# Seeding the attention score banks from ScalarE: three matmul passes instead of four in a post-layernorm transformer block

## The reference, cut to what matters

```python
q, k, v = (hn @ W + b).reshape(b, s, 16, 64)      # q and k then get the rotary embedding
attn = einsum('bihd,bjhd->bhij', q, k) / 8        # causal mask, softmax over j
out = einsum('bhij,bjhd->bihd', softmax(attn), v) @ Wo + bo + h_res
```

## Time and profile before

| | us |
|---|---|
| median of three runs | 2352.92 |
| the profiled execution's own time | 2344.87 |
| its span | 2343.1 |
| PE busy | 2155.6 (92%) |
| DVE busy | 1685.4 (72%) |
| POOL busy | 1433.4 (61%) |
| ACT busy | 957.0 (41%) |

### The profile page before, as it was taken

How to read it: one execution, slowest core, us unless ns; L and a number is a source line. 1 busy time by engine, 2 the same in 40 slices (tenths; PEclk the granted TensorE clock), 3 DMA queues, 4 the chain that set the end, 5 groups by cost and what they waited for, 6 DMA issues and landing times.

```text
span 2343.1 us, 43529 instructions
## 1 busy us (share of the span) xinstructions
PE 2155.6 (92%) x15872; PEld 1415.6 (60%) x15872; DVE 1685.4 (72%) x2313; ACT 957.0 (41%) x1300; POOL 1433.4 (61%) x1204
## 2 busy tenths in 40 slices
PE   5689999999999999899999999999999996898997
PEld 4446565556555655555656565656565654787886
DVE  8567878787878787778787878787878762556544
ACT  3333444344444443334444444343434443334332
POOL 2447777777777777577878787777777785000000
PEclk8799999999999999899999999999999998899998
DMA  5100111011101112101010101010101031212200
GB/s 162 62 19 24 40 31 34 28 38 30 34 27 39 32 33 67 28 24 40 24 40 24 40 24 41 24 41 24 40 24 41 23 109 54 90 64 70 91 9 28
DMA packets 79468, 100.45 MB, mean 43 GB/s; under 512 B 13968, under 2 KB 43664, under 8 KB 78992
## 3 DMA queue, kind: packets, MB, share of 16 engines
q1 hardware_dynamic: 79248, 97.60, 14.0%
HBM read 40.93 MB, written 23.07 MB: 27 GB/s over the span
## 4 chain that ended last, share of the span: by engine, by line
PE 74%; DVE 17%; issue 5%; ACT 1%; DMA 1%; SPq 1%; POOL 0%; DVEq 0%; POOLq 0%; ACTq 0%
PE o_ps L1115 17%; PE m_ps L1063 8%; DVE mpart L731 6%; PE x_ps L1018 6%; PE s_ps L1084 5%; PE x_ps L1020 4%; PE x_ps L1019 4%; PE s_ps L1086 4%; PE s_ps L1090 4%; PE s_ps L1088 4%; PE gu_ps L1018 2%; PE gu_ps L1020 2%; PE gu_ps L1019 2%; PE y_ps L1018 2%; PE x_ps L1122 2%
## 5 line engine op out<-in xcount | busy, mean ns | idle before, releaser
L458 POOL TENSOR_TENSOR acc<-acc,pt 128x512 f32<-128x512 f32 (+3 forms) x1024 | 1233.8, 1236 | 227.0 <-ACT pt L517 226.3
L731 DVE TENSOR_REDUCE mpart<-m_ps 128x2 f32<-128x1024 f32 (+2 forms) x576 | 625.7, 1086 | 346.7 <-PE m_ps L1063 209.7
L517 ACT ACTIVATE pt<-s_ps 128x1024 f32<-128x1024 f32 (+3 forms) x640 | 545.1, 896 | 568.3 <-PE s_ps L1090 319.0
L1115 PE MATMUL o_ps<-pt,v 128*64 128x512 f32 (+3 forms) x2560 | 558.5, 558 | 1.5 <-ACT pt L517 1.5
L1063 PE MATMUL m_ps<-qk 64*128 64x512 f32 (+3 forms) x1280 | 286.1, 442 | 97.2 <-DVE mpart L731 79.4
L1063 PEld LDWEIGHTS m_ps<-qk 64*128 64x128 f32 x1280 | 122.0, 186 | 378.0 <-issue 217.0
L1115 PEld LDWEIGHTS o_ps<-pt,v 128*64 128x64 f32 x2560 | 159.3, 139 | 236.7 <-issue 213.6
L453 POOL TENSOR_TENSOR acc<-pt 128x512 f32<-128x512 f32 (+1 forms) x128 | 165.1, 1310 | 204.1 <-ACT pt L517 204.1
L1084 PE MATMUL s_ps<-qk 64*128 64x512 f32 (+3 forms) x1280 | 249.2, 384 | 0.0
L1086 PE MATMUL s_ps<-qk 64*128 64x512 f32 (+3 forms) x1280 | 235.6, 363 | 0.0
L1090 PE MATMUL s_ps<-aux,ones_r 64*128 64x512 f32 (+3 forms) x1280 | 235.6, 362 | 0.0
(11 more groups left out here) (151 smaller groups left out, 3426.0 us busy)
## 6 DMA issues: line engine op xcount, KB each, us to landing
rot<-qr SPq DMA_DIRECT2D x512, 64.0 KB, 2.0
attn<-o_n SPq DMA_DIRECT2D x64, 256.0 KB, 2.1
o_raw<-attn SPq DMA_DIRECT2D x8, 2048.0 KB, 8.9
w_raw<-in_wqkv SPq DMA_DIRECT2D x51, 128.0 KB, 2.6
h_g<-in_h SPq DMA_DIRECT2D x8, 512.0 KB, 3.5
out<-out_g SPq DMA_DIRECT2D x8, 512.0 KB, 3.2
qk_place<-in_h SPq DMA_DIRECT2D x4, 512.0 KB, 5.5
pt<-in_h SPq DMA_DIRECT2D x4, 512.0 KB, 11.0
```

What stands on the lines that cost most here:

```text
L458: nc.gpsimd.tensor_tensor(sums, sums, probs, ALU.add).then_inc(summed, 1)
L517: nc.scalar.activation(pt[:, u % SLOTS, :, q0:NB], s_ps[:, two:two + 2, q0:NB], ACT.Exp, scale=SCALE)\
L731: nc.vector.tensor_reduce(dst, m_ps[:, :, 0:w], AX.X, ALU.max, negate=True).then_inc(maxed, 1)
L1115: last = nc.tensor.matmul(o_ps[rows, q0:NB], v[par][:, j, rows], pt[:, u % SLOTS, a, q0:NB], start=(j == 0), stop=(j == n - 1), skip_group ...
```

## The change: what it does, and the diff

ScalarE copies the negative maxima into the score banks before a unit's product, and the product's three passes are summed on top (start=False in all of them). The fourth pass, ones and aux are gone. For that the maxima are needed on all 128 partitions, for each head: `turn_maxima` now takes one head at a time, four products of a broadcast column of mc with a rounded identity, and ScalarE copies each head's result into shift. There are two such turns for each block, with `weigh` between them, and the second waits for ScalarE's copy of the first. VectorE's `spread` and mz are gone. ScalarE's `shift_unit` for the two units of group g+1 stands right after the exponentials of group g; each waits for the exponential of the unit that had the bank, and `scores` waits for it. AHEAD goes from 18 to 20, XUSE has another order, and VectorE does cosine and values ahead of turn_sums.

```diff
-AHEAD = 18
+AHEAD = 20
-XUSE = {0: "R3", 1: "M1", 2: "R0", 3: "Q0", 4: "K0", 5: "M2", 6: "R1", 7: "Q1", 8: "K1", 9: "V0", 10: "Q2", 11: "M3",
-        12: "R2", 13: "K2", 14: "V1", 15: "Q3", 16: "V2", 17: "K3", 18: "V3", 19: "M0"}
+XUSE = {3: "Q0", 4: "M20", 5: "K0", 6: "V0", 7: "Q1", 8: "K1", 9: "Q2", 10: "M30", 11: "K2", 12: "V1", 13: "Q3",
+        14: "V2", 15: "K3", 16: "V3", 17: "M01", 19: "M11"}
+SUMMED = {0: 3, 2: 0, 6: 1, 12: 2}
-HN_SPLIT = {1: 0, 4: 1, 8: 2, 12: 3}
+HN_SPLIT = {1: 0, 4: 1, 7: 2, 11: 3}
...
-            def shifts(n, blk):
-                act.wait_ge(m_turned, n * BLOCKS + (blk + 1))
-                nc.scalar.activation(aux[:, :], x_ps[:, :], ACT.Copy).then_inc(aux_done, 1)
+            def shifts(n, blk, a):
+                act.wait_ge(m_turned, n * (2 * BLOCKS) + (2 * blk + a + 1))
+                nc.scalar.activation(shift[:, blk % 2, a, :], x_ps[:, :], ACT.Copy).then_inc(shift_in, 1)
+            def shift_unit(n, u, first=False):
+                blk, j, q0 = UNITS[u]
+                two = 2 * (u % 2)
+                if not first:
+                    act.wait_ge(exped, n * NU + (u - 1))
+                if j <= 1:
+                    act.wait_ge(shift_in, n * (2 * BLOCKS) + 2 * (blk + 1))
+                nc.scalar.activation(s_ps[:, two:two + 2, q0:NB], shift[:, blk % 2, :, q0:NB], ACT.Copy)\
+                  .then_inc(shifted, 1)
...
                     for u in group_units(g):
                         exp_unit(kind, it, u)
+                    for u in group_units(g + 1):
+                        if not first_shift and (u < NU or kind is not LAST):
+                            shift_unit(it + u // NU, u % NU)
...
-                if kind is not FIRST or u >= 2:
-                    pe.wait_ge(exped, it * NU + (u - 1))
+                pe.wait_ge(shifted, it * NU + (u + 1))
...
-                for a, rows in enumerate(halves):
-                    last = nc.tensor.matmul(dst[a], ones_r[rows, :], aux[rows, q0:NB], start=False, stop=not diag)
...
-            def turn_maxima(n, blk):
-                pe.wait_ge(mz_done, n * BLOCKS + (blk + 1))
+            def turn_maxima(n, blk, a):
+                if blk == 0:
+                    pe.wait_ge(maxed, n * NM + TG)
+                else:
+                    pe.wait_ge(m_rows, n * (TT - TG) + TG * blk)
                 for t in range(TG):
-                    last = nc.tensor.transpose(x_ps[:, t * P:(t + 1) * P], mz[:, t, :], id_f[:, :])
+                    last = nc.tensor.matmul(x_ps[:, t * P:(t + 1) * P], mc[:, blk, t, a:a + 1].broadcast_to([P, P]),
+                                            id_r[:, :], start=True, stop=True)
...
+                    if turn is not None:
+                        pe.wait_ge(shift_in, (it + turn[1]) * (2 * BLOCKS) + (2 * turn[0] + 1))
+                        turn_maxima(it + turn[1], turn[0], 1)
```

More of the change, by code:

```diff
@@ L109, in postln_block_kernel @@
         pause = sb("pause", [P, 1], F32)
+        primes = sb("primes", [P, 2], F32)
         with ExitStack() as ctx_attn:
@@ L133, in postln_block_kernel @@
             v1 = sba("v1", [P, TT, P], F32)
-            aux = sba("aux", [P, NB], F32R)
+            shift = sba("shift", [P, 2, 2, NB], F32)
             o_sum = sba("o_sum", [P, NB], F32)
@@ L542, in pair @@
                         piece_hi(it + 1, *PIECE[g - 2], 1 - par)
+                    first_shift = g == 1 and kind is FIRST
                     for u in group_units(g):
                         exp_unit(kind, it, u)
+                    for u in group_units(g + 1):
+                        if not first_shift and (u < NU or kind is not LAST):
+                            shift_unit(it + u // NU, u % NU)
                     if g == 0 and kind is not LAST:
                         weights(it + 1)
-                    if g in TURN_M and (g != NG - 1 or kind is not LAST):
-                        shifts(it + 1 if g == NG - 1 else it, TURN_M[g])
+                    if first_shift:
+                        for a in range(2):
+                            shifts(it, 1, a)
+                        for u in group_units(g + 1):
+                            shift_unit(it, u)
+                    if g in TURN_M and (TURN_M[g][1] == 0 or kind is not LAST):
+                        for a in range(2):
+                            shifts(it + TURN_M[g][1], TURN_M[g][0], a)
                     if g in PIECE and kind is not LAST:
@@ L609, in _ @@
             rounded(3)
-            shifts(0, 0)
+            for a in range(2):
+                shifts(0, 0, a)
             for i in range(TURNS):
                 next_affine(i)
+            act.wait_ge(cos_done, 8)
+            act.wait_ge(banks_whole, 1)
+            for u in range(2):
+                shift_unit(0, u, True)
             each_pair(act, pair)
@@ L812, in pair @@
                 for g in range(NG):
-                    turns = g in TURN_M and (g != NG - 1 or kind is not LAST)
-                    if turns and kind is not FIRST:
-                        spread(it + 1 if g == NG - 1 else it, TURN_M[g])
                     ended = EVICTED.get(g) if g != 1 or kind is not FIRST else None
-                    if ended is not None:
-                        turn_sums(it - 1 if g == 1 else it, ended)
                     if g - 1 in PIECE and kind is not LAST:
@@ L822, in pair @@
                         values(it + 1, VALUES[g - 1], 1 - par, 2)
+                    if ended is not None:
+                        turn_sums(it - 1 if g == 1 else it, ended)
                     for m in group_maxima(kind, g):
-                        maximum(it, m) if m < NM else maximum(it + 1, m - NM)
-                    if turns and kind is FIRST:
-                        spread(it + 1 if g == NG - 1 else it, TURN_M[g])
+                        maximum(it, m, kind is not FIRST) if m < NM else maximum(it + 1, m - NM)
                     if g == 1 and kind is not LAST:
@@ L898, in _ @@
             for m in range(TG):
-                maximum(0, m)
+                maximum(0, m, False)
             turned(2)
             remainders(1)
-            spread(0, 0, first=True)
             unturned(3)
@@ L1160, in pair @@
                         scores(kind, it, par, us[1])
-                    if g in TURN_M and (g != NG - 1 or nxt):
-                        shared_free(g)
-                        turn_maxima(it + 1 if g == NG - 1 else it, TURN_M[g])
+                    turn = TURN_M[g] if g in TURN_M and (TURN_M[g][1] == 0 or nxt) else None
+                    if g == 1 and kind is FIRST:
+                        turn = (1, 0)
+                    if turn is not None:
+                        shared_free(g, 0)
+                        turn_maxima(it + turn[1], turn[0], 0)
                     if g in PIECE and kind is SWITCH:
@@ L1216, in _ @@
             pe.wait_ge(v_done, 4)
+            for i in range(2, 4):
+                last = nc.tensor.matmul(s_ps[:, i, :], id_r[:, :], hn[:, 0, 0, 0:NB], start=True, stop=True)
+            last.then_inc(banks_whole, 1)
             each_pair(pe, pair)
```

94 lines of the change are left out of this document (49 added, 45 removed).

## The result

The changed kernel takes 2513.49 us (median of 4 runs, 2506.04 to 2526.52); the kernel before, run beside it, 2353.82 (4 runs, 2342.64 to 2358.09). The ratio is 1.0694, 95% interval [1.0645, 1.0744]: slower by some 160 us, far above the range that was given. The profiled execution took 2506.04, its span 2504.2.

A forecast was written before the change was run, and what follows sets the result against it. TensorE was taken as the bound, with VectorE's line taking most freed time: 14 regular pairs give -13 us, FIRST and LAST about 0, the head +2, together -11. Predicted 2337 us; the 8-of-10 range was 2265 to 2385.

The forecast's parts named there:

- the wait of group 17: TensorE, between a block's two turns in group 17, waits for ScalarE's first shifts: about 1.2 us idle.
- The sum of a pair: Regular pair: 118.2 us now, 105.0 without idle time and lost clock, 117.3 with the new ones, 0.9 less than now.
- the one in group 5: TensorE's idle 1.45 us in group 5, followed by a 1.2 GHz clock; said to fall away, leaving 0.8 for the clock.
- The removed passes: Dropping the fourth pass of the scores saves TensorE 8.1 us in a pair.
- Where the freed time goes: VectorE's line: TensorE's second maxima or sums come to wait for VectorE: 12.4 us idle in a pair, taken as 11.5.
- the three signs: Forecast wrong if a pair is under 114 us, TensorE's ScalarE waits exceed 3 us a pair, or pairs' clock falls below 0.95.
- VectorE and GpSimd in each other's way: Rival, 0.10: in the denser order VectorE's two-operand steps take their long form, 7 us a pair, half counting: 2391 us.
- TensorE stays the bound: Rival: idle time and clock stay, a pair gains 6.8 us, 2255 us in all; chance 0.22 including a halfway 2295.
- The head: Before the first scores: block 0's second turn, two shift units and one rounding come ahead, +2 us.
- FIRST: First pair, with three and four maxima in a group, held by VectorE: change 0, at most -4 us.
- LAST: Last pair, without projections, GpSimd busy 72.09 of 83 us: change 0, at most -3 us.
- The reading of the first chain: Chain that ended last: 74% TensorE, 17% VectorE, almost all where TensorE waits for a row maximum in two places.

The follow-up runs named there:

- run 8: The kernel before with AHEAD 20 (and FIRST's maxima to match) and nothing else: 2358.55 us, ratio 1.002.
- run 9: The changed kernel with VectorE's V0 and V1 values ahead of the piece's sine and sum in groups 6 and 12: 2491.97 us, ratio 1.0598 to the kernel before.
- run 3: The changed kernel with GpSimd's running additions cut to 8 columns, a block's first two kept whole (sums wrong): 2375.27 us, ratio 1.0122 to the kernel before.
- run 4: The kernel before with GpSimd's running additions cut to 8 columns, a block's first two kept whole (sums wrong): 2292.52 us, ratio 0.9769.
- run 7: The changed kernel with its third pass done twice (scores wrong): 2528.95 us, ratio 1.0762 to the kernel before.
- run 5: The changed kernel with block 1's last turn in group 18 in place of 19: 2516.32 us, ratio 1.0724 to the kernel before.
- run 2: The changed kernel's seeding with the order of the kernel before (old XUSE, AHEAD 18, VectorE's old order): 2490.84 us, ratio 1.0609 to the kernel before.
- run 10: The kernel before with VectorE's cosine and values ahead of turn_sums and nothing else: 2347.28 us, ratio 1.0003.
- run 11: The kernel before with AHEAD 20, turns of blocks 2 and 3 a group earlier, K0 and Q2 in the freed places: 2470.1 us, ratio 1.0524.

## Why the prediction was wrong

**The parts of the change: right, but for the turn.** The shift unit (1.0 us forecast, 1.035 measured), ScalarE's load in a pair (87.5; 414.58 / 5 = 82.9), the seeding hidden (7.1 us of waits in all), the wait of group 17 (1.2; 0.81), AHEAD at nothing (run 8), TensorE's waits for ScalarE below 3 us a pair: all near what was written. The second turn cost 2.3 us a pair and not 1.3: four products take 0.59 us, the upper end of what I gave. The Trainium skill says that ScalarE writes PSUM faster than SBUF ("ScalarE: Activation LUTs", "Step-by-step: what each stage is for"). Nothing of that shows here: the copy of 128x512 into PSUM takes 606 ns, the copy of 128x512 from PSUM into SBUF 598.

```profile
L505 ACT ACTIVATE shift<-x_ps 128x512 f32<-128x512 f32 x128 | 76.6, 598 | 111.8 <-PE x_ps L1123 111.8
L515 ACT ACTIVATE s_ps<-shift 128x512 f32<-128x512 f32 x64 | 38.8, 606 | 0.0
```

**The step that failed: "The sum of a pair".** It says 118.2 - 8.1 + 1.3, without the idle time and the lost clock of now 105.0, plus 11.5 of idle time and 0.8 of lost clock, 117.3. The 13 pairs took 128.2 = 108.2 + 14.6 + 5.3. So of the 10.9 us that are missing, 4.5 are lost clock, 3.2 work and 3.1 idle time.

*The lost clock, 0.8 forecast, 5.3 measured.* I gave it next to nothing because "the one in group 5 falls away". The wait of group 5 did shrink, from 1.45 to about 0.5 us in nine of the 16 pairs; but seven or eight other waits of over 0.8 us came up in a pair, and some of them bring the lower level: of the 57 waits of over 1.5 us in the changed kernel's pairs 22 are followed by 4 us below 0.9, of the 50 between 0.8 and 1.5 us 13. That I let new idle time of 11.5 us come without a clock that falls was the largest error of the sum. Its size is in part luck: waits of the same length and place were followed by the lower level in run 9 and not in the changed kernel.

*The work, 105.0 forecast, 108.2 measured.* The turn is 1.0 of it. The removed passes gave 5.8 us a pair and not 8.1: from start to start, less the waits, the scores of a late pair take 29.7 us where they took 35.5. The issue distances of 0.23 and the like were right; a part of what is missing lies in waits too short to be recorded. In group 6 the second maxima start 0.31 us after the last pass and not 0.23, right behind VectorE's reduction of the first ones, which ended at 1688.60:

```profile
1687.37 1.23 DVE L763 TENSOR_REDUCE mpart<-m_ps 128x2 f32<-128x1024 f32 x1 [0.62 <-PE m_ps L1080]
```
```profile
1688.33 0.40 PE L1106 MATMUL s_ps<-qk 64*128 64x512 f32 x2
1688.64 0.50 PE L1080 MATMUL m_ps<-qk 64*128 64x512 f32 x2
```

In the same place before, the reduction ended at 1556.27, ahead of the start of the last pass at 1556.45. In six groups of the late pairs (3, 6, 7, 12, 15, 16) this distance is 0.32 to 0.51 us, where it was 0.21 to 0.24.

*The idle time, 11.5 forecast, 14.6 measured ("Where the freed time goes: VectorE's line").* Here the walk held rather well, in part by luck, since the durations it was done with are not those that came. In the late pairs, with the forecast behind it: groups 1 and 2 2.5 (2.9), 5 0.8 (1.0), 6 1.6 (1.0), 8 to 11 4.4 (3.8), 12 to 16 1.7 (1.4), 17 0.8 (1.2), 19 1.9 (0.6, without the gap at the loop's jump). It used the mean durations of before's listing, 1.00 + 1.36 + 1.00 us for a piece. These means belong to before's order, in which no sine and sum stood beside a block's first additions. Moving a piece changes which form it takes: K0's sine and sum took 0.68 and 0.69 us in before's group 5 and take 1.67 and 1.64 in group 6, where the values and the sums' turn stand behind them.

So the mechanism was right in part: VectorE's line does take the freed time. What was wrong is the price of its being late. One of the three signs that the prediction named did come: the granted clock of the early pairs is 0.94, below 0.95.

**The rival that held** was "VectorE and GpSimd in each other's way", at 0.10. Its mechanism is the one that runs 3 and 4 show, and the rule of the Trainium skill behind it ("SBUF — State Buffer", "Who interferes with whom") agrees with them: the same step goes from 1.51 to 0.91 us when GpSimd's additions shrink. The size of the effect was too small. I let the steps grow by 7 us a pair, of which half count (4.5 came), and left out that a stopped TensorE may come back slower. The working had a slip besides: it let all three steps grow by the 0.29 us that the sum of 1.36 has left to the long form, while the two others stood at 1.00. Some 80 us of the 163 go away with the additions, and 83 are left, a part of them in groups 6 and 12, where some of the additions are left. "TensorE stays the bound", at 0.22, was the opposite of what came: run 7 shows the removed pass to be worth 15 us, for the 95 that it gave to the passes less the turn.

**What stays open.** The head was to cost +2 and cost 8, FIRST was to cost nothing and cost 10.3; neither was taken apart, but in run 8's trace FIRST is as long with AHEAD 20 alone. LAST, forecast at 0 to -3, is -1.6 together with all that follows it. The gap at the loop's jump is 11 of the 160 us, and its cause is open (run 5). Why the clock falls behind one wait and not behind an equal one is open too. The reading of the first chain was off: VectorE's reductions of the maxima are 5.8% of before's span, a third of VectorE's 17% and not almost all. Two things would test the rest and were not run: a cut of the first additions alone, and an order that hides the seeding and yet keeps groups 5 and 11 free of pieces (run 2 keeps them free, but does not hide it). No version here beats the kernel before; apart from the cut ones, runs 8 and 10 are the same as it.

## What to carry to other kernels

- Price a moved step by its neighbours in its new place, not by its mean: a VectorE step with two operands in SBUF was 0.69 us or 1.65 by whether GpSimd was adding beside it, and two such in front of something that TensorE waits for cost group 7 of run 11 3.8 us, the slow clock behind the wait included.
- A pass taken from the busiest engine is worth what the next wait leaves of it. Before it is removed, look at whether the engine next in line could deliver earlier; here a change of order alone cost 5.2 to 5.8%, and the pass gave 1 us a pair.
- Try a method and the order that it needs as two kernels. Here each half alone cost about 6% and both together 7%.
- Add up idle time, lost clock and work apart. A forecast of new idle time needs a term for the clock: here 9.9 us more idle time in a pair came with 3.4 us more lost clock.

## What the runs showed of the hardware

- After a wait of 1.64 us TensorE's granted clock was 0.57 over the next 4 us, after 2.38 us 0.61; ahead of the first it was 1.00 (1687 to 1691 us, busy throughout). It does not always fall: after a wait of 2.02 us it was 1.00 in the changed kernel, and after one of 2.01 us in the same place 0.50 in run 9. Behind the wait of 1.64 us two products of 512 columns took 0.63 us (1696.83), and 0.40 once the clock was back (1698.04).
- ScalarE copies 128x1024 from SBUF to PSUM in 1.035 us and exponentiates the same from PSUM in 1.023; at 128x512 a copy takes 0.606 us into PSUM and 0.598 out of it.
- A VectorE step with two operands in SBUF (128x512) took 0.68 to 0.69 us, and 1.65 to 1.67 while GpSimd did additions of the same size (run 3, groups 8 and 6).
- A product of 128 columns with a broadcast column of maxima as the weight took 0.147 us on average in a row of four (0.59 us), as long as a transpose of that size took before (0.59 for four).
